# Moving the sigmoid guards of a Mamba-style conv block off VectorE, and a bf16 split onto TensorE

## The reference

```python
def mamba_block(seq, ...):                       # seq: [4, 2304 (+1 token), 128]
    xz = einsum('bld,ed->ble', seq, in_proj_w)   # 512 outputs: u and z, 256 each
    u, z = split(xz, 2)
    u = silu(causal_conv4(u) + conv_b)
    x_dbl = einsum('bld,ed->ble', u, x_proj_w)   # 8 + 16 + 16
    dt, Bm, Cm = split(x_dbl, [8, 24])
    dt = softplus(einsum('blr,dr->bld', dt, dt_proj_w) + dt_proj_b)
    A = -exp(A_log)
    # for each token t:  h = exp(dt*A)*h + dt*u*B ;  y = sum over 16 states of h*C
    y = (ys + u * D) * silu(z)
    return einsum('bld,ed->ble', y, out_proj_w)
...
x = x + mamba_block(pixel_shuffle(layernorm_c(x)))     # x: [4, 512, 24, 24]
t = tokens(x)
t = t + ffn(layernorm_t(t))   # a routed table replaces tokens 1..128 of each image
```

## Time and profile before

| | |
|---|---|
| three runs | 1335.76, 1336.19, 1339.44 us; median 1336.19 |
| the profiled execution | 1343.07 us, of which the span from first to last instruction is 1341.3 |
| granted TensorE clock over the span | 0.94 of full |
| busiest engines | DVE 90%, PE 82%, POOL 81%, ACT 58% |

### The profile page before, as it was taken

One profiled execution on the slowest core, in us unless ns is written; L12 is line 12 of the kernel. 1 busy time (PEld: TensorE's weight loads), 2 busy tenths in 40 slices (PEclk: granted clock), 3 DMA queues, 4 the chain that ended last, 5 costly groups with the idle time before them and its releaser, 6 DMA issues.

```text
span 1341.3 us, 16943 instructions
## 1 busy us (share of the span) xinstructions
PE 1094.4 (82%) x3770; PEld 641.5 (48%) x3770; DVE 1211.3 (90%) x1440; ACT 779.3 (58%) x1423; POOL 1089.0 (81%) x699
## 2 busy tenths in 40 slices
PE   6687888887887887877877877977977888877997
PEld 4343454444444544544544534534534544533887
DVE  1499999999999999999999999999999999999761
ACT  2465665666666666666666656656656656656230
POOL 3288799798898888898898898898897998987850
PEclk9688988999989989989989989989989989888999
DMA  6221221222221221221221222212212213214361
GB/s 155 73 96 48 99 85 68 77 96 78 77 96 62 93 96 54 94 101 55 94 88 67 96 69 86 95 55 100 95 55 100 96 55 116 94 56 140 110 179 30
DMA packets 64537, 116.64 MB, mean 87 GB/s; under 512 B 34218, under 2 KB 47954, under 8 KB 64466
## 3 DMA queue, kind: packets, MB, share of 16 engines
q1 hardware_dynamic: 64466, 115.96, 25.4%
HBM read 108.47 MB, written 7.47 MB: 86 GB/s over the span
## 4 chain that ended last, share of the span: by engine, by line
DVE 44%; issue 21%; PE 18%; ACT 11%; DVEq 3%; POOL 2%; DMA 0%; ACTq 0%; POOLq 0%; SPq 0%
DVE SCAN L936 26%; DVE SCAN L887 8%; PE Yp L672 4%; ACT DA L480 4%; DVE GATES L922 3%; PE PP L701 3%; PE PP L751 3%; POOL SCAN L412 2%; PE PP L716 2%; PE PP L784 2%; DVE VV L898 2%; DVE UDT L1015 2%; DVE GATES L1038 1%; ACT GATES L563 1%; DVE X L1022 1%
## 5 line engine op out<-in xcount | busy, mean ns | idle before, releaser
L412 POOL TENSOR_TENSOR SCAN<-SCAN,CS 128x768 f32<-128x768 f32 x384 | 695.1, 1824 | 99.8 <-DVE SCAN L936 94.3
L936 DVE TENSOR_TENSOR_SCAN SCAN<-DA,CAR,SCAN 128x384 f32<-128x384 f32 x768 | 728.5, 995 | 4.6 <-ACT DA L480 4.0
L672 PE MATMUL Yp<-SCAN,IDENT 128*128 128x384 f32 x1536 | 594.9, 513 | 145.5 <-DVE VV L898 75.8
L480 ACT ACTIVATE DA<-UDT,A 128x384 f32<-128x384 f32 x768 | 442.9, 582 | 446.6 <-DVE SCAN L936 443.6
L672 PEld LDWEIGHTS Yp<-SCAN,IDENT 128*128 128x128 f32 x1536 | 288.5, 198 | 352.2 <-issue 139.5
L887 DVE TENSOR_TENSOR SCAN<-UDT,BB 128x768 f32<-128x768 f32 x288 | 269.0, 934 | 26.8 <-PE BB L654 16.1
L420 POOL TENSOR_TENSOR SCAN<-UDT,BS 128x768 f32<-128x768 f32 x96 | 175.5, 1828 | 0.0
L818 PE MATMUL PP<-XN,WT 128*128 (+1 forms) x384 | 141.8, 505 | 0.2
L654 PE MATMUL BB<-PT,SEL 96*128 96x384 bf16 x288 | 96.6, 336 | 20.3 <-DVE SCAN L887 20.3
L436 POOL TENSOR_TENSOR UDT<-UDT 128x768 f32<-128x768 f32 x24 | 43.4, 1809 | 76.4 <-DVE UDT L1042 76.4
L818 PEld LDWEIGHTS PP<-XN,WT 128*128 128x128 f32 x384 | 73.4, 196 | 59.8 <-issue 16.4
(11 more groups left out here) (156 smaller groups left out, 1130.7 us busy)
## 6 DMA issues: line engine op xcount, KB each, us to landing
CS<-bc_rows SPq DMA_DIRECT2D x96, 768.0 KB, 4.0
BS<-bc_rows SPq DMA_DIRECT2D x24, 768.0 KB, 5.9
out<-XN SPq DMA_DIRECT2D x32, 192.0 KB, 2.5
X<-in_x SPq DMA_DIRECT2D x24, 192.0 KB, 3.4
X<-in_L_ffn_memory_tokens SPq DMA_DIRECT2D x16, 256.0 KB, 3.2
XN<-in_L_ffn_memory_tokens SPq DMA_DIRECT2D x16, 256.0 KB, 3.1
bc_rows<-XDT SPq DMA_DIRECT2D x24, 48.0 KB, 1.5
X<-in_L_ffn_memory_router SPq DMA_DIRECT2D x1, 512.0 KB, 3.5
```

What stands on the lines that cost most here:

```text
L412: pool.tensor_tensor(M[:, n1 % MRING], HB[:, n1 % HRING], over_halves(CS[:, n1 % CRING]), ALU.mult).then_inc(m_ready, 1)
L480: act.activation(DA[:, h, 0:T], DT[:, par, h], ACT.Exp, scale=A[:, h, n:n + 1])\
L672: last = pe.matmul(Yp[:, h, 0:T], IDENT[:, :], M[:, n3 % MRING, h], start=n3 == 0, stop=n3 == NS - 1)
L936: dve.tensor_tensor_scan(HB[:, s % HRING, h], DA[:, h, 0:T], HB[:, s % HRING, h], CAR[:, ds(J * NS * HALVES + s * HALVES + h, 1)], ALU.mul ...
```

## The change

- **B's split.** The two subtractions on VectorE (L908, L1027) go. `LESS` becomes two 96x96 bf16 matrices with -1 on shifted diagonals, and TensorE adds `LESS` times `PART` to `PP` (one matmul of 384 columns in step 4, one in step 5). ScalarE does the three roundings, the last one new (`PT`, step 6).
- **u.** The clamp before the exp (L1015, two instructions) goes. ScalarE takes exp(-(v + bias)) straight from the conv's PSUM, one half at a time (half 0 in step 15 of the unit before, half 1 in step 0). GpSimd clamps the result at 1e19 (a `tensor_scalar` with two operations, in place, 128x768, step 0). The sigmoid stays in `SG`. VectorE forms u = (conv + bias) * sigmoid in one instruction per half (two of 128x384 instead of one of 128x768).
- **z.** The clamp L1034 goes. In step 11 ScalarE takes exp(-z) from PSUM and then copies z to `GZ`; GpSimd clamps the exp in step 12.
- **Loops.** Both hardware loops (units on the compute engines, chunks on SP) are written out.

```diff
-        LESS = sb("LESS", [DTROW, PARTS - 1])
+        LESS = sb("LESS", [DTROW, PARTS - 1, DTROW], BF16)
...
-            with eng.Fori(1, (UNITS - 4) // 2) as i:
+            for i in range(1, (UNITS - 4) // 2):
...
-            with sp.Fori(0, CHUNKS - 1) as c:
+            for c in range(CHUNKS - 1):
... (GpSimd)
+                if front and s == 0:
+                    pool.wait_ge(sg_chain, 2 * f + 1)
+                    pool.tensor_scalar(SG[:, :, :], SG[:, :, :], EXP_LIMIT, 0.0, ALU.min, ALU.max).then_inc(clamped, 1)
                 if main and s + 2 in POOL_STATES:
...
+                if main and s == 12:
+                    pool.wait_ge(sgz_chain, 2 * J + 1)
+                    pool.tensor_scalar(SGZ[:, :, :], SGZ[:, :, :], EXP_LIMIT, 0.0, ALU.min, ALU.max).then_inc(ez_clamped, 1)
... (ScalarE)
-                if front and s == 1:
-                    act.wait_ge(clamped, 2 * f + 2)
-                    positive(act, u_ready, f)
-                    act.activation(SG[:, :, :], U[:, fp], ACT.Exp, scale=-1.0).then_inc(sg_chain, 1)
+                if conv and s == 15:
+                    act.wait_ge(conv_ready, 2 * (J + 2) + 1)
+                    positive(act, u_ready, J + 2)
+                    act.activation(SG[:, 0], PP[:, 0, 0:T], ACT.Exp, bias=NCB[:, 0:1], scale=-1.0)
+                if front and s == 0:
+                    act.wait_ge(conv_ready, 2 * f + 2)
+                    act.activation(SG[:, 1], PP[:, 1, 0:T], ACT.Exp, bias=NCB[:, 1:2], scale=-1.0).then_inc(sg_chain, 1)
...
+                if front and s == 6:
+                    act.wait_ge(res2_ready, f + 1)
+                    act.activation(PT[:, fp], PP[0:DTROW, 1, 0:T], ACT.Copy).then_inc(parts_ready, 1)
...
-                    act.activation(PPT, SG[:, :, :], ACT.Exp, scale=-1.0).then_inc(sg_ready, 1)
+                    act.activation(SG[:, :, :], SG[:, :, :], ACT.Exp, scale=-1.0).then_inc(sg_ready, 1)
...
+                if main and s == 11:
+                    act.wait_ge(z_ready, J + 1)
+                    positive(act, gz_ready, J)
+                    act.activation(SGZ[:, :, :], PPT, ACT.Exp, scale=-1.0).then_inc(sgz_chain, 1)
+                    positive(act, v_ready, J)
+                    act.activation(GZ[:, :, :], PPT, ACT.Copy).then_inc(z_clamped, 1)
... (TensorE)
+                if front and s == 4:
+                    pe.wait_ge(hi_ready, f + 1)
+                    pe.matmul(PP[0:DTROW, 1, 0:T], LESS[:, 0], PART[:, :], start=False, stop=False,
+                              skip_group_check=True).then_inc(res_ready, 1)
+                if front and s == 5:
+                    pe.wait_ge(mid_ready, f + 1)
+                    pe.matmul(PP[0:DTROW, 1, 0:T], LESS[:, 1], PART[:, :], start=False, stop=True,
+                              skip_group_check=True).then_inc(res2_ready, 1)
... (VectorE)
-                    dve.tensor_tensor(U[:, fp], U[:, fp], PPT, ALU.mult).then_inc(u_ready, 1)
+                    for h in range(HALVES):
+                        last = dve.scalar_tensor_tensor(out=U[:, fp, h], in0=PP[:, h, 0:T], scalar=CB_[:, h:h + 1],
+                                                        in1=SG[:, h], op0=ALU.add, op1=ALU.mult)
+                    last.then_inc(u_ready, 1)
...
-                        dve.tensor_scalar(U[:, fp, h], PP[:, h, 0:T], CB_[:, h:h + 1], NEG_LIMIT, ALU.add, ALU.max)\
...
-                    dve.tensor_scalar(GZ[:, :, :], PPT, NEG_LIMIT, None, ALU.max).then_inc(z_clamped, 1)
```

More of the change, by code:

```diff
@@ L34 @@
 NEG_LIMIT = -44.0
+EXP_LIMIT = 1.0e19
 EPS_C, EPS_T = 1e-6, 1e-5
@@ L458, in weights @@
                 act.activation(A[:, :, :], AE[:, :, :], ACT.Exp).then_inc(set_act, 1)
+                act.activation(NCB[:, :], CB_[:, :], ACT.Copy, scale=-1.0)
                 act.wait_ge(set_act, 1)
@@ L598, in step @@
                     act.activation(SQ[:, :, :], XC[:, :, :], ACT.Square).then_inc(sq_ready, 1)
-                if main and s == 13:
-                    act.wait_ge(z_clamped, J + 1)
-                    positive(act, gz_ready, J)
-                    act.activation(SGZ[:, :, :], GZ[:, :, :], ACT.Exp, scale=-1.0).then_inc(sgz_chain, 1)
                 if norm and s == 12:
@@ L856, in weights @@
                     dve.tensor_scalar(DD[:, h], IDENT[:, :], DV[:, h:h + 1], None, ALU.mult)
-                dve.memset(LESS[:, :], 0.0).then_inc(less_set, 1)
+                dve.memset(LESS[:, :, :], 0.0).then_inc(less_set, 1)
                 dve.wait_ge(less_set, 1)
-                dve.memset(LESS[BC:2 * BC, 0:1], -1.0)
-                dve.memset(LESS[2 * BC:3 * BC, :], -1.0).then_inc(less_set, 1)
-                dve.wait_ge(less_set, 2)
+                for part in range(1, PARTS):
+                    rows = slice(part * BC, (part + 1) * BC)
+                    for step in range(part):
+                        last = dve.tensor_scalar(LESS[rows, step], IDENT[rows, 0:DTROW], -1.0, None, ALU.mult)
+                last.then_inc(less_set, 1)
             X0v = X[:, 0:BATCH * T].rearrange("p (b q t) -> p q b t", b=BATCH, q=Q)[:, :, :, 0]
@@ L904, in step @@
                         drive(J + 1, 1 - par, 0, N + 1)
-                if front and s == 6:
-                    dve.wait_ge(hi_ready, f + 1)
-                    dve.scalar_tensor_tensor(out=PP[0:DTROW, 1, 0:T], in0=PART[:, :], scalar=LESS[:, 0:1],
-                                             in1=PP[0:DTROW, 1, 0:T], op0=ALU.mult, op1=ALU.add)\
-                        .then_inc(res_ready, 1)
                 if back and s == 10:
@@ L1010, in step @@
                     weigh(3)
-                if front and s == 0:
-                    for h in range(HALVES):
-                        dve.wait_ge(conv_ready, 2 * f + h + 1)
-                        dve.tensor_scalar(U[:, fp, h], PP[:, h, 0:T], CB_[:, h:h + 1], NEG_LIMIT, ALU.add, ALU.max)\
-                            .then_inc(clamped, 1)
                 if back and s == 5:
@@ L1023, in step @@
                     last.then_inc(x2_ready, 1)
-                if front and s == 6:
-                    dve.wait_ge(mid_ready, f + 1)
-                    dve.scalar_tensor_tensor(out=PT[:, fp], in0=PART[:, :], scalar=LESS[:, 1:2],
-                                             in1=PP[0:DTROW, 1, 0:T], op0=ALU.mult, op1=ALU.add)\
-                        .then_inc(parts_ready, 1)
-                if main and s == 11:
-                    dve.wait_ge(z_ready, J + 1)
-                    if back:
-                        dve.wait_ge(v_ready, k + 1)
-                    dve.tensor_scalar(GZ[:, :, :], PPT, NEG_LIMIT, None, ALU.max).then_inc(z_clamped, 1)
                 if front and s == 13:
```

15 lines of the change are left out of this document (8 added, 7 removed).

## The result

The changed kernel takes 1303.05 us (four runs, 1301.56 to 1304.42) against 1336.42 for the kernel before on the same chip: ratio 0.9733, 95% interval 0.9707 to 0.9760 (the two medians alone give 0.9750), so 33 us less where 20 were forecast, and below the forecast's own range of 1309 to 1325. The profiled execution took 1302.34.

A forecast was written before the change was run, and what follows sets the result against it. VectorE and GpSimd were both taken as tight, with GpSimd's chain holding the changed unit at 50.25 us against 51.15; 0.9 us over 22 units gives 19.8, so 1336.2 - 19.8 = 1316.4, said as 1316, range 1309 to 1325.

The forecast's parts named there:

- VectorE's 2.7 us: Work taken off VectorE per unit (clamps, B's subtractions, less u's growth): about 2.7 of 50.16 us, turning into waits for GpSimd.
- TensorE's stall: Between scans 3 and 5 of unclean units: waits of 0.59 and 0.32 us, to be covered by waiting for GpSimd.
- VectorE's stall at the turn: At the hardware loop's turn VectorE stands still for 1.24 us; writing out was to remove it.
- Where the two meet: Walk through a clean unit on VectorE and GpSimd with the clamps added: it comes out at 50.25 us, not 47.4.
- The first step: GpSimd's back-to-back stretch behind the first clamp, up to L420 for state 9: all of it ends 0.85 us later.
- The second step: Ahead of L918: its 0.45 us wait for TensorE's mean absorbs most of scan 9's 0.57 delay, leaving scan 10 0.1 late.
- Some 6 us lower: The forecast result if a GpSimd clamp took 0.64 us, estimated from its 1.2 GHz clock, instead of 0.85.
- rival 1: Step 13: L922 goes ahead of GpSimd's L412; a unit takes about 49.65 us, 1303 us in all; chance 0.20.
- The prediction's own sign: In the changed kernel's profile, L922's successor (VectorE's softplus step) would still take near 1.9 us.
- Rival 2: GpSimd's clamps cost what a two-input operation does, 1.82 us; a unit takes about 51.3 us, 1339 in all; chance 0.13.
- rival 3: TensorE as new bound through the B chain, residual add of step 5 late; 51.55 us a unit, 1345; chance 0.11.
- rival 4: The unclean units' stalls stay, moved behind scan 9 or otherwise caused; 51.2 us a unit, 1337, no change; chance 0.08.

The follow-up runs named there:

- e5: The changed kernel with B's split back on VectorE (two subtractions in step 6; ScalarE's third rounding and TensorE's two matmuls gone): 1311.63 us.
- e6: The changed kernel with z's clamp back on VectorE, ScalarE's two PSUM reads and GpSimd's second clamp taken away: 1309.67 us.
- e12: The changed kernel with state 3's drive moved from GpSimd to VectorE, BB's buffer index getting the unit's parity: 1288.34 us.
- e7: The changed kernel with GpSimd's clamp of u's exp done twice: 1324.46 us.
- e3: The changed kernel without both of GpSimd's clamps of the exp (overflow guard left out): 1269.71 us.
- e8: The changed kernel with the hardware loops back on all engines but GpSimd, which stays written out: 1306.53 us.
- e9: The changed kernel with all hardware loops back, a tiny GpSimd product ahead of each clamp taking over its wait: 1318.09 us.
- e1: The kernel before with its two hardware loops written out and nothing else: 1329.94 us.
- e4: The changed kernel with GpSimd's product of state 12 made to wait until VectorE's softplus step L951 is done: 1293.22 us.
- e11: The kernel before, written out, with B's split on TensorE and ScalarE as in the change and nothing else of it: 1304.70 us.

## Why the prediction was right or wrong

**Right in its frame.** VectorE's 2.7 us did for the most part turn into waits for GpSimd, 1.74 ahead of the scans and 0.57 inside L951, and only 0.49 came out of a clean unit (50.16 to 49.67). e5, e6 and e12 exclude VectorE's busy time as the bound of the middle units, e7 and e3 show GpSimd's clamps in full. TensorE's stall is covered by these waits, as B's arrival shows. VectorE's stall at the turn is gone too, but e8 shows that no cover is needed for that in the changed kernel. The clamps, 0.79 to 0.83, were taken at 0.85.

**Wrong in size: 50.25 a unit, measured 49.67.** Two steps of "Where the two meet" failed: that all of GpSimd's stretch ends 0.85 later, and that L918's wait takes in the delay and leaves scan 10 0.1 late. The 0.58 us that they are off make 12.8 us in 22 units, of the 13.4 by which the forecast missed. The first step: counted from dt*u's start, L425 for state 9 ends at 31.44 us (626.04 + 1.82 - 596.42) against 30.96 in the earlier trace rows: 0.48 later and not 0.85. 0.06 of the difference is the clamp's price. 0.31 is GpSimd's looped form: from L450 to the next L413 it takes 1.33 us, and in the looped unit of before 1.64, from 622.67 to the 624.31 of the earlier trace rows (timeline of POOL, before):

```profile
622.67 1.11 POOL L441 TENSOR_TENSOR XN<-XC,RSTD 128x192 f32 x2
624.04 0.19 POOL L444 COPY XN<-XN  x1 [0.26 <-POOL XN L441]
```

The prediction gave the written-out form to VectorE alone ("written out, there is no turn"), and not to GpSimd, which by its own argument set the pace. e8 and e9 show that the 0.31 goes with GpSimd's loop and comes out in full.

**The wait for TensorE's mean.** The second step let the 0.45 us ahead of L918 take in 0.57 and left 0.1 over, as if the mean came at a fixed time. It comes from TensorE, whose matmuls for it stand behind those of another mean (L737), and these wait for ScalarE's reads of PSUM, which in turn stand behind the decays of scan 8 (timelines of ACT, then PE, then PE of before):

```profile
627.59 0.80 ACT L583 ACTIVATE UDT<-PP 128x768 f32<-128x768 f32 x1
```

```profile
628.54 1.10 PE L737 MATMUL PP<-X,MEANW 128*128 128x96 f32 x8 [0.35 <-ACT UDT L583]
```

```profile
649.25 1.13 PE L716 MATMUL PP<-X,MEANW 128*128 x8 [1.56 <-ACT UDT L564]
```

VectorE does scans 7 and 8 0.66 us sooner, those matmuls start 32.12 us behind dt*u's start instead of 32.85, and no wait is left: L947 stands 34.63 us behind it, formerly 35.02. Of the 0.45, writing out alone takes 0.2 (e1); e5, with scan 8 late again, has the other 0.23 back. Together with the clamps' price and the 0.31 this is the whole of the 0.6 us by which the product of state 12 comes earlier than forecast (43.20 against 43.71 before, forecast 43.8). What follows L951's end is as forecast: 3.83 us to the next dt*u, 3.82 before.

**The units at the ends.** I gave all 22 the gain of the middle. By L1042 and L1056, the first interval went from 46.01 to 42.54, the second from 50.93 to 48.72 and the last from 53.74 to 49.01. There GpSimd lacks work of other units, or VectorE has the routed FFN's, so that VectorE's 2.7 us can count in full; no run tests this.

**Size of the sum.** In the two profiled executions the spans differ by 40.7 us, in the runs by 33.4. Of the 40.7, the two intervals at either end give 11.7 and the 19 between them 28.7. The profiled execution of before was 6.9 us above its median, that of the changed kernel 0.7 below: the 6.9 belongs to that one execution of before. Which units it sat in can't be told, so the 51.15 us and the gains read against it can be up to 0.3 us a unit too high, and that 12.8 of the 13.4 us come out of the middle units is in part luck. "Some 6 us lower" for a clamp of 0.64 us doesn't follow from the prediction's own steps either: scan 9 would be 0.36 late, L918's wait takes that in, and 0.1 us a unit, 2 us, is all that goes.

**The rivals.** The time is that of rival 1 (49.65 a unit, 1303), and that is chance, for its mechanism didn't occur: it needed L922's successor to go ahead of the product, at 0.96, and it takes 2.51. The prediction's own sign, a duration near 1.9, failed too; its rule held, the end of L951 hangs on GpSimd's product, but L951 is now issued sooner against it. The near tie was real (0.13 us), and e4 shows that the other order would have given 10 us more. Rival 2 falls with the clamps at 0.83, rival 3 with no wait of the residual add for TensorE, rival 4 with intervals that are all alike. The part-by-part view missed that the split alone, on written-out units, is worth as much as everything (e11): u and z take work from VectorE and give GpSimd 1.58 us that come out nearly in full (e3), and the two cancel over the program, with a loss in the middle units and a gain at the ends.

## What to carry to other kernels

When two engines take turns as the one that is waited for, follow one unit on both timelines and mark where each has no idle time: work taken from the one is worth only the slack of the other, and here moving one product of 1.81 us back from the relieving engine to the "busiest" one made the kernel faster. Price a moved guard at the place where it lands in an in-order queue, and every side effect of a rewrite (address arithmetic, loop turns) on the engine that holds the pace. A wait that looks like slack may move with the work in front of it.

## What was not expected of the hardware

- A VectorE instruction with two SBUF inputs can be 0.96, 1.33, 1.76, 1.95 or 2.51 us long for the same 128x768, by what GpSimd has in hand when it is issued; the wait is inside the duration and appears in no idle time. It works the other way too: GpSimd's second norm (128x384) takes 1.71 us in the kernel before, where it starts under L922, and 1.00 in the changed kernel. Making GpSimd wait instead gained 10 us. The Trainium skill (SBUF — State Buffer, Who interferes with whom) calls it an exclusive lock, and these rows agree.
- A `tensor_scalar` with two operations on GpSimd, 128x768 float32, takes 0.83 us, against 1.82 for a product of two inputs.
- What a hardware loop costs depends on the kernel around it. In the kernel before, VectorE stood still for 1.24 to 1.43 us at each turn; with the same loops in the changed kernel (e8, e9) it didn't. In both, GpSimd's looped form took 0.31 us more in each unit, and a scan of VectorE that GpSimd released began 0.24 to 0.26 us later instead of 0.03 to 0.04 (e8).
